# The steps of a token group in another order, in the instruction lists of all engines of a delta-rule and mixture-of-experts layer

## The reference

```python
x = x + attn(layernorm(x))      # gated delta rule, 8 heads of 128x128
x = x + moe(layernorm(x))       # 8 experts of 128-512-128, the best 2 for each token
# attn: q, k, v = split(causal_conv4(x @ qkv_w.T)); beta = sigmoid(x @ b_w.T); alpha = exp(-exp(A_log) * softplus(...))
# for each token t:  S = S * alpha_t
#                    S = S + k_t (v_t - k_t S) * beta_t
#                    o_t = q_t S
# o = rmsnorm(o) * norm_w * silu(x @ z_w.T); out = o @ out_w.T
```

## Time and profile before

| | us |
|---|---|
| median of 3 executions | 1405.44 |
| lowest, highest | 1398.91, 1411.79 |
| the profiled execution | 1402.14 |
| its span, first to last instruction | 1400.3 |

### The profile page before, as it was taken

How to read it: one execution, slowest core, us unless ns; L and a number is a source line. 1 busy time by engine, 2 the same in 40 slices (tenths; PEclk the granted TensorE clock), 3 DMA queues, 4 the chain that set the end, 5 groups by cost and what they waited for, 6 DMA issues and landing times.

```text
span 1400.3 us, 38612 instructions
## 1 busy us (share of the span) xinstructions
PE 1179.3 (84%) x13898; PEld 1039.7 (74%) x13898; DVE 1035.5 (74%) x2501; ACT 939.4 (67%) x2864; POOL 773.1 (55%) x725
## 2 busy tenths in 40 slices
PE   1369999989898989898999899999999985488881
PEld 1147888878787879797878787888888885376771
DVE  5686878787778787787868786869797826666655
ACT  3356868687767778686868676868686854266663
POOL 2147374848475756566665656575848442254551
PEclk9988999999989899999979898989999967699996
DMA  5122222222222221212121313221222241422214
GB/s 148 46 48 64 39 64 49 61 50 76 47 60 52 55 61 46 62 45 62 45 69 38 77 29 77 34 73 35 76 40 68 49 130 58 120 64 65 61 50 180
DMA packets 230893, 90.06 MB, mean 64 GB/s; under 512 B 184471, under 2 KB 218141, under 8 KB 229812
## 3 DMA queue, kind: packets, MB, share of 16 engines
q1 hardware_dynamic: 191012, 73.36, 21.4%
q10 hardware_dynamic: 35152, 5.78, 2.2%
q0 software_dynamic: 4544, 8.47, 1.9%
HBM read 66.77 MB, written 23.83 MB: 65 GB/s over the span
## 4 chain that ended last, share of the span: by engine, by line
PE 55%; DVE 20%; ACT 11%; issue 8%; another core or an unknown queue 2%; DMA 2%; SPq 1%; POOL 1%; ACTq 0%; DVEq 0%; POOLq 0%
PE rc L1701 5%; PE kx L1642 4%; PE rc L1710 4%; PE ob L1729 4%; PE ob L1730 4%; PE rc L1718 3%; PE kx L1552 3%; DVE tapA L1199 3%; PE pj L1654 3%; DVE area L1202 2%; PE rc L1692 2%; ACT Gs L880 2%; PE pj L1656 2%; PE pj L1655 2%
## 5 line engine op out<-in xcount | busy, mean ns | idle before, releaser
L652 POOL TENSOR_TENSOR kq<-tapA,area 128x256 f32<-128x256 f32 x256 | 228.7, 902 | 157.9 <-DVE area L1202 157.0
L790 ACT ACTIVATE area<-pj,taps 128x256 f32<-128x256 f32 x384 | 183.3, 477 | 174.6 <-PE pj L1656 156.5
L1199 DVE SCALAR_TENSOR_TENSOR tapA<-pj,taps,tapA 128x256 f32<-128x256 f32 x384 | 184.4, 480 | 134.6 <-ACT tapA L790 126.7
L790 ACT ACTIVATE tapA<-pj,taps 128x256 f32<-128x256 f32 x384 | 183.3, 477 | 0.0
L1202 DVE SCALAR_TENSOR_TENSOR area<-pj,taps,area 128x256 f32<-128x256 f32 x384 | 182.7, 476 | 0.0
L632 POOL TENSOR_TENSOR kq<-kq,area 128x1024 f32<-128x1024 f32 x64 | 166.5, 2603 | 0.0
L652 POOL TENSOR_TENSOR vT<-tapA,area 128x256 f32<-128x256 f32 x128 | 91.2, 731 | 135.9 <-DVE area L1202 134.0
L1654 PE MATMUL pj<-xn_hi,w_hi 128*128 128x259 f16 x384 | 113.9, 297 | 49.8 <-DVE area L1202 33.3
L1642 PE MATMUL kx<-kq 128*128 128x128 f32 x1024 | 145.9, 288 | 0.3 <-ACT area L801 0.3
L1642 PEld LDWEIGHTS kx<-kq 128*128 128x128 f32 x1024 | 132.0, 202 | 8.9 <-issue 5.4
L681 POOL DMA_INDIRECT rows_out<-rhs,e_dst x78 | 82.6, 1059 | 90.9 <-ACT rhs L933 38.0
(11 more groups left out here) (310 smaller groups left out, 3653.3 us busy)
## 6 DMA issues: line engine op xcount, KB each, us to landing
area<-scr_alpha SPq DMA_DIRECT2D x32, 512.0 KB, 3.7
area<-scr_acum SPq DMA_DIRECT2D x32, 512.0 KB, 3.8
area<-rows_in SPq DMA_DIRECT2D x39, 130.0 KB
scr_n<-area SPq DMA_DIRECT2D x128, 32.0 KB, 1.7
area<-rows_out SPq DMA_DIRECT2D x4, 1024.0 KB, 8.3
rows_in<-rows_in SPq DMA_DIRECT2D x8, 260.0 KB
kq<-in_x SPq DMA_DIRECT2D x4, 512.0 KB, 11.0
blkN<-scr_n SPq DMA_DIRECT2D x32, 64.0 KB, 2.7
```

The costliest lines, as they stand in the source:

```text
L652: nc.gpsimd.tensor_tensor(dst[:, n % H, :], tapA[:, n % RING, :], tapB[:, n % RING, :], ALU.add).then_inc(conv_done, 1)
L790: ins = nc.scalar.activation(dst[:, n % RING, :], pj[n % 2][:, k:k + GT], ACT.Copy, scale=taps[:, t, k:k + 1])
L1199: nc.vector.scalar_tensor_tensor(out=tapA[:, n % RING, :], in0=pj[n % 2][:, 0:GT], scalar=taps[:, order[n], 0:1], in1=tapA[:, n % RING, :] ...
```

## The change

The string `ORDER` is replaced by another that holds the same 260 names. Nothing else is changed: no instruction is added, removed or given another shape.

```diff
-            proj.0 taps.0 first.0 ka.0 proj.1 taps.1 first.1 y16 ye first.2 xl.0 last.0 proj.2 taps.2 re v.0.0
-            taps.3 td.0 r16 aq.0 taps.4 proj.3 first.3 v.0.1 me.1.0 td.1 last.1 ks.0.0 me.0.0 first.4 al.0 proj.4
-            taps.5 first.5 last.2 ks.0.1 me.1.1 scan.0 m.1.0 me.0.1 m.0.0 first.6 diag.0 me.1.2 proj.5 first.7 m.1.1
-            taps.6 first.8 last.3 ac.0 m.0.1 rhs.0.0 nm.0.0 proj.6 taps.7 first.9 last.4 m.1.2 me.0.2 proj.7 nm.0.1
-            rhs.0.1 m.0.2 last.5 scan.1 me.1.3 m.1.3 nm.1.0 al.1 taps.8 kk.0.0 last.6 nm.1.1 proj.8 me.0.3 first.10
-            m.0.3 taps.9 last.7 proj.9 first.11 ue.0.0 kk.0.1 st.0.0 taps.10 u.0.0 diag.1 g.0.0 sm no.0 proj.10
-            first.12 ue.0.1 kk.1.0 sp.0 st.0.1 proj.11 taps.11 u.0.1 first.13 s2 last.8 kk.1.1 first.14 sq.0.0
-            sd.0.0 g.0.1 taps.12 no.1 o.0.0 aq.1 first.15 taps.13 sd.0.1 inv.0 taps.14 proj.12 last.9 proj.13 inv.1
-            sq.0.1 o.0.1 zg.0.0 taps.15 last.10 proj.14 inv.2 rhs.1.0 bi ktr.0.0 rhs.1.1 inv.3 v.1.0 last.11 scale.0
-            inv.4 proj.15 zt.0.0 inv.5 v.1.1 ka.1 ks.1.0 ue.1.0 inv.6 ks.1.1 ue.1.1 zg.0.1 last.12 z.0.0 xl.1 kd.0.0
-            inv.7 z.0.1 zt.0.1 g.1.0 u.1.0 last.13 sq.1.0 inv.8 u.1.1 kd.0.1 o.1.0 rms.0 last.14 ktr.0.1 sq.1.1
-            rms.1 o.1.1 ac.1 scale.1 zg.1.0 sp.1 ktr.1.0 kd.1.0 g.1.1 sd.1.0 zt.1.0 at.0.0 ktr.1.1 last.15 kd.1.1
-            z.1.0 inv.9 gn.0.0 sd.1.1 zg.1.1 nr kq.0.0 zt.1.1 to at.0.1 z.1.1 gn.0.1 inv.10 last.16 kq.0.1 gte.0.0
-            first.16 proj.16 taps.16 gt.0.0 last.17 first.17 taps.17 proj.17 rk gte.0.1 xt ti last.18 first.18 xe
-            gt.0.1 first.19 lg tp last.19 x2.0 proj.18 gn.1.0 proj.19 ps taps.18 out.0 sc first.20 taps.19 gt.1.0
-            xs.0 first.21 gn.1.1 proj.20 last.20 st.1.0 gte.1.0 pf at.1.0 proj.21 taps.20 last.21 gt.1.1 first.22
-            taps.21 kq.1.0 first.23 gte.1.1 proj.22 last.22 xs.1 x2.1 tj kq.1.1 st.1.1 taps.22 proj.23 last.23
-            at.1.1 taps.23 out.1
+            proj.0 taps.0 first.0 ka.0 y16 ye first.1 proj.1 taps.1 re xl.0 last.0 proj.2 taps.2 first.2 r16 sm td.0
+            v.0.0 diag.0 taps.3 proj.3 td.1 ks.0.0 taps.4 first.3 last.1 proj.4 me.1.0 scan.0 al.0 v.0.1 me.0.0
+            first.4 last.2 m.1.0 taps.5 first.5 m.0.0 me.1.1 proj.5 first.6 last.3 me.0.1 m.1.1 first.7 m.0.1 me.1.2
+            nm.0.0 aq.0 ac.0 ks.0.1 taps.6 first.8 m.1.2 taps.7 nm.0.1 last.4 proj.6 me.0.2 proj.7 first.9 rhs.0.0
+            m.0.2 last.5 scan.1 me.1.3 m.1.3 nm.1.0 xl.1 taps.8 kk.0.0 last.6 nm.1.1 proj.8 me.0.3 st.0.0 m.0.3
+            rhs.0.1 last.7 proj.9 first.10 taps.9 kk.0.1 first.11 taps.10 u.0.0 diag.1 first.12 ue.0.0 al.1 kk.1.0
+            st.0.1 ue.0.1 proj.10 sp.0 first.13 u.0.1 taps.11 kk.1.1 first.14 sq.0.0 last.8 sd.0.0 inv.0 taps.12
+            o.0.0 inv.1 scale.0 no.0 ktr.0.0 ka.1 inv.2 taps.13 proj.11 inv.3 rhs.1.0 v.1.0 last.9 proj.12 g.0.0
+            taps.14 sd.0.1 inv.4 rhs.1.1 aq.1 ks.1.0 g.0.1 kd.0.0 no.1 proj.13 sq.0.1 inv.5 v.1.1 last.10 ue.1.0
+            inv.6 proj.14 taps.15 first.15 ks.1.1 last.11 o.0.1 scale.1 inv.7 proj.15 zt.0.0 zg.0.0 last.12 z.0.0 bi
+            ue.1.1 inv.8 u.1.0 kd.0.1 inv.9 u.1.1 last.13 sq.1.0 g.1.0 ktr.0.1 s2 o.1.0 rms.0 last.14 o.1.1 sq.1.1
+            rms.1 ktr.1.0 ac.1 kd.1.0 zg.0.1 sp.1 sd.1.0 kd.1.1 zg.1.0 sd.1.1 zt.0.1 at.0.0 ktr.1.1 last.15 zt.1.0
+            z.0.1 g.1.1 gn.0.0 z.1.0 inv.10 nr kq.0.0 gn.0.1 to zg.1.1 z.1.1 zt.1.1 first.16 last.16 gt.0.0 gte.0.0
+            at.0.1 proj.16 gte.0.1 gt.0.1 last.17 first.17 taps.16 xt rk tp proj.17 ti last.18 first.18 taps.17
+            kq.0.1 x2.0 proj.18 xe sc ps lg gn.1.0 proj.19 first.19 taps.18 out.0 last.19 first.20 gn.1.1 gt.1.0
+            xs.0 at.1.0 taps.19 pf last.20 st.1.0 gte.1.0 proj.20 first.21 gt.1.1 taps.20 last.21 kq.1.0 first.22
+            gte.1.1 proj.21 x2.1 tj kq.1.1 last.22 xs.1 st.1.1 taps.21 proj.22 at.1.1 taps.22 out.1 last.23 first.23
+            taps.23 proj.23
```

## The result

The changed kernel took 1439.8 us in the median of four runs (1432.71 to 1451.09), the kernel before beside it 1407.49: ratio 1.0258, with an interval of 1.0214 to 1.0303. It is slower by 2.6%, where "no change" was forecast; the time lies just under the upper end of the range. In a later comparison on another chip, where the kernel before took 1359.05 us, the ratio was 1.0317 (1.0259 to 1.0375). The profiled execution after took 1444.12 us, its span is 1442.3.

A forecast was written before the change was run, and what follows sets the result against it. No engine alone was taken to bound the kernel: PE bounds the turn's middle, two latency chains its length. Terms (1) to (5) summed to nothing, (6) to 0.5 us over 15 turns, +7: 1409 us, range 1375 to 1440.

The forecast's parts named there:

- Step (1): Turn's start: the inverse's chain starts sooner, `re` at 6.5 for 7.14 us, `u.0.0` 1.5 to 2 us sooner.
- Step (2): Convolutions pushed back behind the inverse: the 1.5 to 2 us are waited away; `first.14` ends 0.2 us sooner.
- Step (3): DVE's chain: substitution 1.84 us sooner behind `first.14`, its stretch to the end of `rms.1` 2.0 us longer; net nothing.
- Step (6): POOL against DVE: `sp.1` and the substitution's products hold each other up, 0.5 us a turn, +7 us in all.
- the upper price: Upper bound on the extra wait of DVE and POOL: `sp.1` whole, 1.9, less 0.5, so 1.4 us a turn.
- today's share: The 0.5 us of `inv.1` that the old order already loses beside `sp.1`.
- the nearest row: Profile row of `inv.1`, 0.98 us beside `sp.1`; its stall gave the 0.5 us a turn assumed.
- Step (5): Turn's end: `sc` starts 0.7 us sooner, but `last.19` stands behind it, so `last.20` and `taps.0` stay; nothing.
- B: Rival: `sp.1` costs 1.4 us a turn, `scan.1` behind `ka.1` 2.1 us in half the turns; 1439 us, chance 0.22.
- C: Rival: PE's low clock lasts 4 us longer over full work, 2 us a turn; 1432 us, chance 0.07.
- A: Rival: the sooner inverse is kept, 1.5 us a turn gained; 1379 us, chance 0.32.

The follow-up runs named there:

- its clock held up: Changed kernel with six added matmuls of 512 columns a turn in PE's waits: 1.0146 of the kernel before; with `proj.11` and `taps.11` also put back, 1.0036.
- the fillers: Six added matmuls of 512 columns a turn where PE waits: 0.9802 in the kernel before, 1.0146 in the changed kernel.
- the first filling: Changed kernel with three added matmuls of 512 columns ahead of `proj.1`, where PE waits after `y16`: 1.0443 of the kernel before.

## Why the prediction was wrong

**Step (1) failed, in sign.** It had `re` sooner, 6.5 for 7.14, and `u.0.0` 1.5 to 2 us sooner. In the mean `re` came 1.57 us later behind `y16` and `u.0.0` 0.93 later. Three things were left out. First, `ye` does not hang on `y16`: it starts 7.2 us behind the start of `sc` in both orders, since ACT first does two `taps` whose start hangs on what comes behind `sc`. `y16` did start 0.5 us sooner behind `sc`, and nothing came of it. Second, `r16` ran at the low clock (3.1 to 3.6 us in 12 of 13 turns, median 3.6, for 2.7 before; 0.7 us in the mean), a price that the 0.57 of the earlier trace rows hints at and that I left out of the sum. Third, `r16` still stands behind `proj.2`, and that behind `first.0`, which DVE reaches after one more convolution step; this held it 0.4 us, and nothing in the changed kernel on the other chip, where `r16` starts 0.2 us behind the end of `ye` as it does before. Counted from `sc`, `re` is 1.1 us later (12.98 for 11.85), and these last two are all of it. What I had right is that the moves behind `re` save time: 0.64 us of the 1.3 that my two numbers imply.

**Step (2) was right in itself.** `u.0.0` to `first.14` was to grow by what (1) gained, 1.5 to 2 us; it grew 2.02, and PE waits 1.1 us for `st.0.1` in each turn. With (1) gone there was nothing to net it with. That is the step of the sum that cost the forecast: two terms of 1.5 to 2 us with opposite signs were put at nothing together, though each hung on other waits. Together (1) and (2) were to end 0.2 us sooner and ended 2.95 later, nearly the whole 3.05 us of the turn. `proj.11` alone, one of the names moved, costs 1.9% in the kernel before and 1.1% in the changed one with its clock held up.

**Step (3)** had -1.76 (I said -1.84) right. The stretch to the end of `rms.1` I took as +2.0, and +2.5 with (6); it was +2.85. That this is near is in part luck: without `sp.1` the stretch is 12.37 us, so the steps moved into it cost 1.5, not 2.0, and `sp.1` 1.4, not 0.5.

**Step (6) was mis-sized**: 0.5 us taken, 1.4 measured when `sp.1` was taken away (13.75 to 12.37 us), just the upper price that I gave. I had reached it by taking off today's share of 0.5, but today's share fell into slack and wasn't to be taken off; instead the product starts 0.4 us behind `sp.1`, and that much is not lost. The value of the nearest row came from a product that `sp.1` met in its second half; the new order lets it meet a product of 0.16 us early, which then lasts as long as `sp.1` does. The Trainium skill ("SBUF — State Buffer", "Who interferes with whom") says that the later of the two is blocked to the other's end; the pair 1.97 and 1.58 us, the second starting 0.40 behind the first, agrees with it in most turns, as did `scan.1` behind `ka.1` at 4.42. I should have taken its result for the sum, since no work of DVE stood between. I also misread `last.5`: by its row it ended at 666.45, 0.5 us behind `scan.0` and not with it.

**Step (5)** was right in effect: an old end within the new order brings nothing. The end of `rms.1` to `sc` fell by 0.46 us, for 0.7 expected. `first.0` does start 1.2 us later behind `y16` in the mean (3.44 for 2.20), but `y16` itself starts 0.5 us sooner behind `sc`; what that order costs is in step (1).

**The rivals.** B gave 1439 and the time was 1439.8, but half by another way: `sp.1` as said, `scan.1` at over 4 us in 4 turns of 13 (2 before), not in half, and the rest by the pushback. C was taken as the clock staying low longer; in three turns it did (17 us), but the mean didn't change, and yet the fillers gave the kernel before 2.0% and the changed one 1.7% (1.0317 to 1.0146). A found no support: no order that was run without fillers and with the whole `sp.1` was faster than the one before.

## What to carry to other kernels

When an order is changed, don't net a gain against a loss because they are alike in size: write down for each which wait it hangs on, and ask what the time is if one of them does not come. Follow each step of a gained chain through the engine's list, too: starting `y16` sooner gained nothing, for `ye` stood behind two steps that wait for the last engine to finish the turn. Where a short DVE product between two SBUF tiles and a long POOL instruction over SBUF can start together, price it at all that is then left of the longer one. A few matmuls of filling in PE's waits can be worth more than an order, but look in the turn's trace at where the clock is low afterwards: the first filling of the changed order moved the low stretch onto full work and lost 1.2% (1.0317 to 1.0443), while the same three matmuls gained 0.9% in the kernel before.

## What the runs showed of the hardware

The same kernel took 1402.6 us on one chip and 1359 to 1364 on three others. Most of such a difference lies behind the last `y16`, in the expert work: the windows from there to the end, changed kernel on the first and on another chip:

```profile
1164.00:1442.30 278.30, 191.44 (x2171) 162.88 (x2170) 160.64 (x402) 146.91 (x381) 111.05 (x104) 0.86 0.32 92
```

```profile
1155.30:1398.70 243.40, 178.87 (x2175) 160.40 (x2174) 161.37 (x402) 151.69 (x381) 107.21 (x105) 0.84 0.36 105
```

278.3 us against 243.4, 34.9 less at no higher clock, where the whole span is 43.6 us less. On the first chip `x2.1` also started late behind the end of `out.1`, at the time when POOL issues its indirect transfers. `out.1` and the `x2.1` that waits for it, beside `sc`, on the first chip and on the other:

```profile
739.34 1.95 PE L1744 MATMUL ob<-ow,GTs 128*128 128x128 f32 x16
...
741.67 0.97 POOL L621 DMA_INDIRECT rows_in<-rowbuf,dest  x1 [0.30 <-issue]
...
743.57 0.29 DVE L1280 TENSOR_TENSOR xres<-ob,xres 128x128 f32<-128x128 f32 x1 [1.95 <-remote]
```

```profile
734.91 1.95 PE L1744 MATMUL ob<-ow,GTs 128*128 128x128 f32 x16
...
735.98 0.97 POOL L621 DMA_INDIRECT rows_in<-rowbuf,dest  x1 [0.30 <-issue]
...
736.97 0.29 DVE L1280 TENSOR_TENSOR xres<-ob,xres 128x128 f32<-128x128 f32 x1
```

2.28 us behind `out.1`'s end on the one, 0.11 on the other. In the 13 turns it is 1.0 to 2.4 us on the first chip, and 2.2 or more in 12 of them; on the other it is 0.11 in most and 0.7 at most. In the kernel before it was late on the first chip too. What makes the two chips differ stays open.
